# Rows of every second pair turned by VectorE and exchanged through DRAM, in the first and the last expert loop

## What is computed

```python
# cond0: 8 experts of width 128; _leaky(z) = where(z >= 0, z, 0.01 * z)
y_all = einsum('etm,emh->eth', _leaky(x @ w_gate[e]) * (x @ w_up[e]), w_down)
y = sum over the 2 chosen experts of weight * y_all, + a shared expert
# ffn0: 8 experts of width 512: gelu(x @ W1[e] + b1[e]) @ W2[e] + b2[e]
# cond1: attention of 16 heads with a bias, between two layer norms
# ffn1: 16 experts of width 128
h = silu(x @ w1[e].T + b1[e]) * (x @ w3[e].T + b3[e])
y = y + gatew[:, e:e+1] * (h @ w2[e].T + b2[e])
y = y + a shared expert of width 256
```

## Time and profile before

| | |
|---|---|
| median of 3 runs | 786.5 us (785.26 to 789.51) |
| profiled execution | 780.06 us, its span 778.2 us |
| first loop in the span | from 42 to 119 us |
| last loop in the span | from 660 to 752 us |
| TensorE, VectorE, ScalarE, GpSimd busy | 90%, 61%, 51%, 55% |

### The profile page before, as it was taken

The page is one execution under the profiler, slowest core; times in us unless marked ns, Lnnn a source line. Parts: engine busy times, 40 slices in busy tenths (PEclk is TensorE's granted clock), DMA queues, the critical chain, the costliest instruction groups (busy, mean ns, idle before and its releaser), DMA issues. The chain is left out here.

```text
span 778.2 us, 15602 instructions
## 1 busy us (share of the span) xinstructions
PE 700.5 (90%) x4389; PEld 544.4 (70%) x4390; DVE 471.2 (61%) x1730; ACT 395.0 (51%) x1100; POOL 430.8 (55%) x540
## 2 busy tenths in 40 slices
PE   8878998675899999998799999899999989998986
PEld 5457995455699999986566666566666654887865
DVE  1722457267444445424888888899998945354546
ACT  4444651124344444424767657576766625765611
POOL 1075604560555685243876877898896654255550
PEclk9897999795699999999999999999999999999999
DMA  9834534345377777541899999888888773455428
GB/s 324 315 95 117 156 106 132 102 132 207 103 228 228 219 219 203 158 148 58 305 312 343 317 351 327 297 295 270 306 266 298 267 282 106 123 148 151 132 80 320
DMA packets 120813, 166.22 MB, mean 214 GB/s; under 512 B 29984, under 2 KB 97056, under 8 KB 119840
## 3 DMA queue, kind: packets, MB, share of 16 engines
q1 hardware_dynamic: 103632, 127.65, 49.3%
q0 software_dynamic: 10944, 30.03, 12.5%
q10 hardware_dynamic: 6160, 7.64, 3.0%
HBM read 100.07 MB, written 65.21 MB: 212 GB/s over the span
## 5 line engine op out<-in xcount | busy, mean ns | idle before, releaser
L1849 ACT ACTIVATE work<-work 128x129 f32<-128x129 f32 (+1 forms) x256 | 114.4, 448 | 73.7 <-DVE work L1986 72.6
L2011 DVE STREAM_TRANSPOSE region_bd<-work 128x384 f32<-128x384 f32 x128 | 73.1, 571 | 13.4 <-DMA c_blocks<-region_bd 9.3
L1430 POOL DMA_INDIRECT d_pairs<-work,home x47 | 47.6, 1012 | 52.5 <-DVE home_f L1180 35.3
L1595 PE MATMUL psY<-work,region_ac 128*128 128x256 f32 x256 | 70.0, 396 | 3.8 <-ACT work L1843 3.8
L2306 POOL TENSOR_TENSOR work<-region_bd,region_ac 128x386 f32<-128x386 f32 x64 | 59.6, 939 | 19.1 <-DVE work L1986 11.1
L1419 POOL DMA_INDIRECT b_pairs<-work,home x39 | 38.1, 976 | 56.7 <-DVE work L1124 54.6
L2306 POOL TENSOR_TENSOR work<-work,region_ac 128x386 f32<-128x386 f32 x64 | 59.6, 943 | 17.3 <-DVE work L1986 9.3
L1411 POOL DMA_INDIRECT work<-in_x,inv x39 | 37.2, 953 | 56.0 <-DVE inv L1337 36.0
L1633 PE MATMUL psM<-region_ac,work 128*128 128x256 f32 x256 | 66.9, 384 | 0.0
L1082 ACT ACTIVATE work<-work 128x512 f32<-128x512 f32 x39 | 24.6, 630 | 80.5 <-issue 46.9
L1622 PE MATMUL psL<-region_bd,work 128*64 128x256 f32 (+1 forms) x512 | 55.8, 338 | 7.2 <-DVE work L2020 3.9
(11 more groups left out here) (392 smaller groups left out, 1649.5 us busy)
## 6 DMA issues: line engine op xcount, KB each, us to landing
c_blocks<-region_bd SPq DMA_DIRECT2D x64, 512.0 KB
region_bd<-c_blocks SPq DMA_DIRECT2D x64, 512.0 KB
work<-d_rows SPq DMA_DIRECT2D x47, 132.0 KB
a_slots<-work SPq DMA_DIRECT2D x19, 256.0 KB
b_turned<-work SPq DMA_DIRECT2D x35, 128.0 KB
work<-b_turned SPq DMA_DIRECT2D x35, 128.0 KB
region_bd<-in_b_w SPq DMA_DIRECT2D x1, 3072.0 KB, 21.5
region_ac<-in_fside SPq DMA_DIRECT2D x12, 256.0 KB
```

What stands on the lines that cost most here:

```text
L1430: pool.indirect_dma_start(out=st.pair_dram, out_offset=bass.IndirectOffsetOnAxis(ap=home[:, t:t + 1], axis=0), in_=d_ys[:, t % ROWS, :], i ...
L1595: last = pe.matmul(psY[:, 0:SEQ], c_wq[:, c, j * P:(j + 1) * P], c_xnT[:, odd, c, :], start=(c == 0), stop=(c == KD - 1))
L1849: nc.scalar.activation(c_p[:, j % 2, o, a:z], c_sc[:, o, a:z], ACT.Exp, scale=-1.0, bias=c_min[:, o, i:i + 1], accum_out=c_sum[:, j % 2, o ...
L2011: nc.vector.transpose(out=c_x1[:, p % 2, :, (QT + 1) * o:(QT + 1) * (o + 1), :].rearrange("p b i q -> p i b q"), in_=c_p[:, j % 2, o, 1:1 ...
```

## The change

Some pairs are exchanged: those with odd number from 5 on, but not the last pair (`exchanged`). For these TensorE has no turn and ScalarE no copy_x. In step p VectorE turns blocks for pair p+4 (`x_blocks`, `EARLY = 4`), as its last work of the step but the shared product. SyncE stores them (`sp_store_x`), waits until they are stored and the pair three before is through its first product, and loads them into the place where copy_x would have put them (`sp_load_x`). TensorE's in(p) then waits for that load. In the first loop SyncE's store for pair p+7 and load for pair p+6 stand behind the slot store of pair p, those of pair 5 ahead of all slot stores. In the last loop they stand behind the loads of the rows of pair p+2 and p+3. The ring of rows in the last loop becomes ten tiles deep, and homes runs a pair ahead. Loads of rows that overwrite an exchanged pair wait for `x_blocks` in place of `turned`; `turned`, `xT_ready` are counted by `by_pe`, `x_blocks` is one semaphore for all three loops.

```diff
--- before.py
+++ after.py
@@ -47,6 +47,9 @@
 LAST_BANKS = 8
 ADDED_FIRST = 6
 FIRST_HALVES = 4
+ROWS_D = 10
+FIRST_EXCHANGED = 5
+EARLY = 4
 TURNED = 4
 AHEAD = 4
 KEPT_W1 = 3
@@ -163,10 +166,22 @@
         self.h_gate = sem(f"{name}_h_gate") if kind == "leaky" else None
         self.h_ready = sem(f"{name}_h_ready")
         self.w_ready = sem(f"{name}_w_ready")
-        self.x_blocks = sem(f"{name}_x_blocks") if kind == "gelu" else None
+        self.x_blocks, self.blocks_from = None, 0
         self.behind = 1 if kind == "silu" else 2
         self.y_mm = sem(f"{name}_y_mm")
         self.y_out = sem(f"{name}_y_out")
+    def exchanged(self, p):
+        return p % 2 == 1 and FIRST_EXCHANGED <= p < self.outs - 1
+    def ex(self, p):
+        return sum(self.exchanged(q) for q in range(p))
+    def by_pe(self, p):
+        return max(p, 0) - self.ex(p)
 class Shared:
...
@@ -885,7 +907,7 @@
             experts = Experts(pe, f)
             def turn(p):
-                wait(pe, f.xT_ready, p - DEEP + 1)
+                wait(pe, f.xT_ready, f.by_pe(p - DEEP + 1))
                 for t in f.tiles(p):
                     pe.wait_ge(*rows_landed(f, 0, t))
                     for k in range(KD):
@@ -893,13 +915,17 @@
                 last.then_inc(f.turned, 1)
             def products_in(p):
-                pe.wait_ge(f.xT_ready, p + 1)
+                if f.exchanged(p):
+                    wait_dma(pe, f.x_loaded, 0, f.ex(p))
+                else:
+                    pe.wait_ge(f.xT_ready, f.by_pe(p) + 1)
                 wait(pe, f.h_ready, p - DEEP + 1)
                 for t in f.tiles(p):
                     pe.wait_ge(f.w_ready, t + 1)
                     for j in range(2):
                         for k in range(KD):
-                            last = pe.matmul(pair_h[p % DEEP][:, t % PAIR, j, :], f.w_in(j, k, t), xT[:, p % DEEP, t % PAIR, k, :],
+                            rows_T = xTe[:, p % DEEP, :, t % PAIR, k, :] if f.exchanged(p) else xT[:, p % DEEP, t % PAIR, k, :]
+                            last = pe.matmul(pair_h[p % DEEP][:, t % PAIR, j, :], f.w_in(j, k, t), rows_T,
                                              start=(k == 0), stop=(k == KD - 1))
                 last.then_inc(f.h_mm, 1)
@@ -928,7 +954,7 @@
             for p in range(1, f.outs + f.behind):
                 if f.st is D and p <= 2:
                     pe.wait_ge(D.shared.part_ready, 14 + p)
-                if p + 1 < f.outs:
+                if p + 1 < f.outs and not f.exchanged(p + 1):
                     turn(p + 1)
                 if p < f.outs:
                     products_in(p)
@@ -1013,7 +1039,7 @@
             def copy_x(p):
                 n = len(f.tiles(p))
-                act.wait_ge(f.turned, p + 1)
+                act.wait_ge(f.turned, f.by_pe(p) + 1)
                 wait(act, f.h_mm, p - DEEP + 1)
                 nc.scalar.copy(xT[:, p % DEEP, 0:n, :, :], pair_x[p % DEEP][:, 0:n, :, :]).then_inc(f.xT_ready, 1)
@@ -1048,13 +1074,13 @@
                 act_shared_halves(act, 15, 16)
             place_w(2)
             for p in range(f.outs):
-                if f.st is A and p + 2 < f.outs:
+                if f.st is A and p + 2 < f.outs and not f.exchanged(p + 2):
                     copy_x(p + 2)
                 fetch(p + 3)
                 gate(p)
                 if p + 3 < f.outs:
                     place_w(p + 3)
-                if f.st is D and p + 2 < f.outs:
+                if f.st is D and p + 2 < f.outs and not f.exchanged(p + 2):
                     copy_x(p + 2)
                 if f.st is D and p in KEPT_AT:
                     act_shared_silu(act, D.shared, KEPT_AT.index(p))
@@ -1175,22 +1201,39 @@
                 for t in f.tiles(p):
                     dve.wait_ge(*rows_landed(f, 0, t))
-                n, t, at = len(f.tiles(p)), PAIR * p, PAIR * p % ROWS
+                n, t, at = len(f.tiles(p)), PAIR * p, PAIR * p % ROWS_D
                 ids = d_rows[:, at:at + n, DIM:DIM + 1].rearrange("p r o -> p (r o)")
                 nc.vector.tensor_tensor(home_f[:, t:t + n], ids, inv_c[:, 0, t:t + n], ALU.mult).then_inc(D.homed, 1)
                 dve.wait_ge(D.homed, 2 * p + 1)
                 nc.vector.scalar_tensor_tensor(out=home[:, t:t + n], in0=home_f[:, t:t + n], scalar=-1.0, in1=inv_c[:, 1, t:t + n],
                                                op0=ALU.add, op1=ALU.add).then_inc(D.homed, 1)
+            def x_blocks(p):
+                n = f.ex(p)
+                for t in f.tiles(p):
+                    dve.wait_ge(*rows_landed(f, 0, t))
+                if n >= 2:
+                    wait_dma(dve, f.x_stored, 0, n - 2)
+                for t in f.tiles(p):
+                    last = nc.vector.transpose(out=f.x1[:, n % 2, :, t % PAIR, :, :],
+                                               in_=slot_rows(f, t).rearrange("p (k q b) -> p b k q", k=KD, b=4))
+                last.then_inc(f.x_blocks, 1)
             fetch(0)
+            if f.st is D:
+                homes(0)
             for p in range(f.outs + f.behind):
                 if p < f.outs:
-                    if f.st is D:
-                        homes(p)
+                    if f.st is D and p + 1 < f.outs:
+                        homes(p + 1)
                     gated(p)
                 if p >= f.behind:
                     results(p - f.behind)
                 fetch(p + 1)
+                if f.exchanged(p + EARLY):
+                    x_blocks(p + EARLY)
                 if f.st is D and p - 1 in KEPT_AT:
                     dve_shared_gated(dve, D.shared, KEPT_AT.index(p - 1))
@@ -1393,6 +1436,14 @@
+        def wait_rows_turned(eng, f, p):
+            if f.exchanged(p):
+                eng.wait_ge(f.x_blocks, f.blocks_from + f.ex(p) + 1)
+            else:
+                eng.wait_ge(f.turned, f.by_pe(p) + 1)
         def pool_gather_rows(pool, st, first, last):
             f = st.ffn
@@ -1402,11 +1453,11 @@
                     wait_dmas(pool, st.token_stored)
             for t in range(first, last):
                 if st is B and t >= ROWS + TURNED:
-                    pool.wait_ge(f.x_blocks, t - ROWS - TURNED + 1)
+                    pool.wait_ge(f.x_blocks, f.blocks_from + t - ROWS - TURNED + 1)
                 elif st is B and t >= ROWS:
                     pool.wait_ge(f.turned, t - ROWS + 1)
                 elif st is A and t >= ROWS_DEEP:
-                    pool.wait_ge(f.turned, (t - ROWS_DEEP) // PAIR + 1)
+                    wait_rows_turned(pool, f, (t - ROWS_DEEP) // PAIR)
                 landed, _ = rows_landed(f, 0, t)
                 pool.indirect_dma_start(out=slot_rows(f, t), out_offset=None, in_=st.src,
                                         in_offset=bass.IndirectOffsetOnAxis(ap=inv[:, t:t + 1], axis=0)).then_inc(landed, 16)
...
@@ -1488,6 +1539,29 @@
                 elif n < BIAS_LOADS + OTHER_LOADS:
                     load_other(sp, x_tiles, n - BIAS_LOADS)
+        def sp_store_x(sp, f, p):
+            if f.exchanged(p):
+                n = f.ex(p)
+                sp.wait_ge(f.x_blocks, f.blocks_from + n + 1)
+                if n >= 2:
+                    wait_dma(sp, f.x_loaded, 0, n - 2)
+                sp.dma_start(f.x_dram[n % 2].rearrange("a (k b) m -> (a k) (b m)", b=4),
+                             f.x1[:, n % 2, :, :, :, :].rearrange("p b i k q -> p (b i k q)")).then_inc(f.x_stored.sems[0], 16)
+        def sp_load_x(sp, f, p):
+            if f.exchanged(p):
+                n = f.ex(p)
+                wait_dma(sp, f.x_stored, 0, n)
+                sp.wait_ge(f.h_mm, p - DEEP + 1)
+                if n >= 1:
+                    wait_dma(sp, f.x_loaded, 0, n - 1)
+                sp.dma_start(xTe[:, p % DEEP, :, :, :, :].rearrange("p a i k q -> p a (i k q)"), f.x_dram[n % 2].rearrange("a s m -> s a m")
+                             ).then_inc(f.x_loaded.sems[0], 16)
         def sp_load_rows(sp, st):
@@ -1495,14 +1569,17 @@
             sp.wait_ge(*st.experts)
             wait_dmas(sp, st.dispatched)
             at = [sp.alloc_register(f"{f.name}_start{r}") for r in range(RING)]
-            for t in range(f.n):
-                if t >= ROWS:
-                    p = (t - ROWS) // PAIR
-                    sp.wait_ge(f.turned, p + 1)
-                    sp.wait_ge(st.homed, 2 * p + 2)
-                sp.reg_load(at[t % RING], tile_start[0:1, t:t + 1])
-                row = sp.snap(at[t % RING], min_val=0, max_val=16 * TOKENS - P)
-                sp.dma_start(d_rows[:, t % ROWS, :], d_in[bass.ds(row, P), :]).then_inc(f.loaded.sems[t % ROWS], 16)
+            for m in range(f.outs + 2):
+                for t in f.tiles(m):
+                    if t >= ROWS_D:
+                        p = (t - ROWS_D) // PAIR
+                        wait_rows_turned(sp, f, p)
+                        sp.wait_ge(st.homed, 2 * p + 2)
+                    sp.reg_load(at[t % RING], tile_start[0:1, t:t + 1])
```

(12 more changed lines are left out.)

15 lines of the change are left out of this document (11 added, 4 removed).

## The result

The changed kernel takes 790.42 us (median of 22 runs, 786.72 to 799.45), the kernel before 786.57 us (22 runs, 781.73 to 790.72). The ratio is 1.0045, interval 1.0027 to 1.0062: 3.9 us slower, where 3.7 us faster was forecast. The time lies 0.4 us above the range.

A forecast was written before the change was run, and what follows sets the result against it. The prediction took TensorE to bound the first loop and late even gates the last. Last loop 4.0 gained, first loop 3.1 - 2.0 - 1.4 = -0.3: 3.7 us off the 786.5 median, 782.8 us, range 776 to 790.

The forecast's parts named there:

- What bounds the loops: Both loops: TensorE full in the first, 3.09 us a step; late even gates hold the last, 7.46 us per two steps.
- The removals, 7.1 us: Both loops: each turn taken off TensorE gains 0.44 us, 3.1 us in the first and 4.0 in the last.
- The additions at nothing: Both loops: VectorE's added transposes, 1.29 us a pair, and SyncE's two more DMAs fit in idle time and cost nothing.
- The round trip, 5.8 us: Store plus load of an exchanged pair takes 5.8 us, ends 4.6 and 9.4, plus 0.2 for SyncE's waking.
- The chain ahead of it in the first loop, 4.2 us from in(P-4)'s end to the transposes' end: First loop: gate, results, copy and VectorE's transposes before the store take 4.2 us, between 3.4 and 6.1.
- The landing's cost in the first loop, 2.0 + 1.4 us: First loop: TensorE waits 0.7 us for exchanged rows three times, 2.0 us, and 1.4 us at pair 5.
- Last loop: landed in time by 0.4, gain 4.0: Last loop: rows land 11.7 us after in(P-4), needed after 12.1, so the turns' full 4.0 us is gained.
- Slower: Rival, both loops: the exchange becomes the bound at in(P); a 7.5 us round trip gives 795 us; chance 0.17.
- from 6.9 us on: Both loops: the round trip from which the rival of a slower kernel decides, 0.5% slower.
- The landings eat it all: Rival, both loops: late landings use up the gain, nothing left at a round trip of about 6.5 us, 786 us; chance 0.20.
- The late gates: Rival, last loop: even gates come in time, so TensorE's 8.0 us of waiting goes too, 775 us; chance 0.15.
- the price of VectorE's work: Both loops: the skill's rule read as 16 x 1.29 us added for 7.1 removed, 800 us, only where VectorE's fit fails.

The follow-up runs named there:

- e3: Kernel before with turns and copies of the sixteen pairs left out in both loops, nothing in their place; first level, ratio 0.9937 to the kernel before.
- e6: Kernel before with the first loop's seven turns and copies left out, nothing in their place; second level, ratio 0.9996 to the kernel before.
- e4: Kernel before plus VectorE's transposes, stores and loads in both loops; TensorE still turns every pair, no product waits; first level, ratio 1.0032.
- e17: Changed kernel with the exchange in the first loop alone, landing waits kept, results in a ring of four pairs; first level, 1.0099 to the kernel before.
- e1: Changed kernel with the exchange kept in the first loop alone, TensorE turning every pair of the last; first level, 1.0098 to the kernel before.
- e14: Changed kernel, exchange in the first loop alone, products reading earlier turned rows and waiting for no landing; second level, 1.0110 to the kernel before.
- e16: First loop's exchange alone, no product waiting for a landing, results in a ring of four pairs; first level, 1.0002 to the kernel before.
- e2: Changed kernel with the exchange kept in the last loop alone, TensorE turning every first-loop pair; first level, 0.9951 to the kernel before.
- e18: Exchange in the last loop alone, its transposes, store and load each one step sooner than in the changed kernel; first level, 0.9986 to the kernel before.
- e13: Exchange in the last loop alone, its transposes, store and load each one step sooner than in the changed kernel; second level, 1.0007 to the kernel before.
- e9: The changed kernel once more, nothing else altered, on a chip of the second level; ratio 1.0185 to the kernel before.
- e10: The kernel before, unchanged, run a second time in one group on the second level; ratio 0.9977 to itself.

## Why the prediction was wrong, point by point

- **What bounds the loops.** Right for the chip that was read: first loop full, last loop held by late gates. That the gates are late on one level of chips only could not be seen in one trace. That they are late in the first loop too, while GpSimd's gathers run, could have been looked for there: the chain of pair 7 hangs on such a gate.
- **The removals, 7.1 us.** Measured 4.9 (e3). First loop: the steps of 2.65 and 3.09 us came exactly (e6), but the kernel gained at most 2.2 us of them.
- **The additions at nothing.** 2.5 us (e4), at the edge of what could be told. SyncE's two DMAs do not delay rows, as said; they delay slot stores, which was not asked. On the first level that costs nothing as long as the landing waits stand (e17 against e1). On the second it is what is left when they are gone (e14).
- **The round trip, 5.8 us.** Right as a mean, 6.1 over seven pairs: in the changed kernel's first loop the transposes' end to the landing was 4.8 to 5.6 us at pairs 5, 11, 13 and 17. But it was used as one number. Pair 9 had 7.1 us, hidden because pair 7 had already held the loop up, and pairs 7 and 15 had 6.5 and 8.4 us to TensorE's release.
- **The chain ahead of it in the first loop, 4.2 us from in(P-4)'s end to the transposes' end.** It was 7.6 and 6.6 at pairs 7 and 9, 3.8 and 3.9 at 11 and 13, 4.2 at 15, 6.3 at 17: 5.4 in the mean, and above the upper end of 6.1 at three of six pairs. (Its lower end is 3.3 by the prediction's own terms, not 3.4.)
- **The landing's cost in the first loop, 2.0 + 1.4 us.** This is the step that failed: the term has the right wait, but its 3.4 us are less than half of the 7.6 measured (e16 against e17). It came from 4.2 + 6.0 = 10.2 us against 9.5, the same at each pair, so every wait after pair 5's was 0.7. The changed kernel's profile has 14.1 us at pair 7, where the late gate made the chain long, and 12.6 at pair 15, where the store took 5.4, while TensorE wanted the rows after 11.1 and 10.5; the other pairs landed in time or nearly so, and what a late pair costs is not given back by an early one. The forecast also had nothing for the clock. In the changed kernel's profile it cost 1.8 us behind each of two waits, in e17's nothing, so the 7.6 divides into 5.1 of waiting and a rest that the runs don't place.
- **Last loop: landed in time by 0.4, gain 4.0.** Its landings were in time, and e2 measured 3.8, e18 1.1. On the second level, with 6.18 us for two steps, the same term is a loss of 2.8.
- **The rivals.** "Slower" named the right wait, and an exchange bound by its round trip in both loops at 7.5 us; it came in one loop, at single pairs. The point "from 6.9 us on" was passed there at pairs 9 and 15 alone. "The landings eat it all" was nearest in size. The late gates did not go. The Trainium skill's rule from VectorE: DVE Perf Modes, Rules for kernel authors (turn 128 by 128 on TensorE where PSUM will do), came out right for the first loop and for the second level, but not by the price of VectorE's work that I had given it. At that price e16 would lose 7 x 1.29 = 9.0 us for 3.1 of turns, and it came out within 0.3% of the kernel before; so no run bears that price out, while in e13 the fuller VectorE does hold gates back.

## What to carry to other kernels

When work is moved off the engine that bounds a loop and the result comes back through DRAM, compare the spread of the route with the time there is, pair by pair, and not its mean: a wait of the bounding engine is paid in full, and in some executions again in clock. Where two waits can stand in for each other, take away both before saying what either costs. List what stands behind each new wait in the in-order queue that carries the transfers, and who waits for that. And where a profile has idle time that nothing explains, a gain or loss that rests on it may be one chip's: here the same last-loop edit was worth -0.5% on one and +0.4% on another.

## What the runs showed of the hardware

- **Two levels of chips.** The kernel before took 783 to 787 us in three groups of runs and 741 to 743 in three others, on two chips. On the second level all steps of the loops were 3.09 us, and the step from in(2) to in(3) took 3.09 us where it was 12.5 on the first. On the second, the gates of pairs 4 to 22 of the last loop start 0.14 us after their product ended (once 0.44); on the first, up to 3.2 us after it in the kernel before, and in the changed kernel's first loop once 4.6, 4.47 of it by no worker the profile knows. Why the levels differ is open.
- **The clock after a short wait.** In the changed kernel's profile TensorE ran at its lower level for about 3 us behind waits of 2.93 and 2.15 us, and in e1's behind one of 2.44. Behind waits of 3.13 us in e17 and 2.82 in e9 it did not: the product that had waited took 2.05 us. Behind the first loop it always waits 0.5 to 1.8 us for the last results; after one of 1.7 to 1.8 us in e3, e4, e9 and e10 the next four matmuls of 512 columns took 3.4 to 3.6 us, after the same wait in e2, e6 and e14 they took 1.98. What decides it between them is open.
- **One transfer of 256 KB varies.** In the changed kernel's first loop stores took 2.0 to 5.4 us; the 5.4 fell where the DMA engines also carried GpSimd's gathers. The queues from 100 to 104 us (packets, MB, share of the engines' time) are below: the gathers' queue took more of the engines for fewer bytes. On the second level, with DMA shares of 0.75 to 0.83 in the last loop, stores of 3 to 5 us were common.

```profile
q0 software_dynamic: 86, 0.22, 51.0%
q1 hardware_dynamic: 396, 0.47, 32.2%
```
